# Moving weight loads of a Mamba and FFN layer from SyncE's DMA queue to ScalarE's and GpSimd's

## The reference, cut to what matters

```python
xn = layernorm(x)                                   # 16384 tokens, d_model 1024
# branch 1: a selective state space block, d_inner 2048, 16 states, chunks of 256 tokens
xr = xn @ W_in.T + b_in                             # 1024 -> 4096, split into xc and res
u = silu(causal_conv3(xc) + conv_b)
dlt, Bm, Cm = split(u @ W_x.T, [64, 80])
delta = softplus(dlt @ W_dt.T + b_dt)
carry = exp(delta * -exp(A_log)) * carry + delta * Bm * u     # scan within a chunk, carry 0 at its start
y = sum_over_states(carry * Cm) * silu(res)
ssm = y @ W_out.T + b_out                           # 2048 -> 1024
# branch 2: a gated FFN of 4096, activations rounded to 8 bits, weights to three values
ffn = bitlinear(silu(bitlinear(xn, w_gate)) * bitlinear(xn, w_up), w_down)
out = x + ssm + ffn
```

## Time and profile before

| | |
|---|---|
| time, median of 10 runs | 5199.13 us (5194.39 to 5205.92) |
| time of the profiled execution | 5196.19 us |
| its span on the slowest core (core 0) | 5194.5 us |
| spans of the 8 cores | 5150.0 to 5194.5 us |
| DVE busy | 3800.2 us, 73% of the span |
| ACT, PE busy | 1858.3 us (36%), 1604.3 us (31%) |
| POOL busy | 100.2 us (2%) |
| DMA bytes by queue | SP 316.68 MB, POOL 46.15 MB, ACT 12.58 MB |

### The profile page before, as it was taken

How to read it: one execution, slowest core, us unless ns; L and a number is a source line. 1 busy time by engine, 2 the same in 40 slices (tenths; PEclk the granted TensorE clock), 3 DMA queues, 4 the chain that set the end, 5 groups by cost and what they waited for, 6 DMA issues and landing times.

```text
span 5194.5 us, 46593 instructions; the slowest of 8 cores (5150.0 to 5194.5 us)
## 1 busy us (share of the span) xinstructions
PE 1604.3 (31%) x7308; PEld 812.5 (16%) x7308; DVE 3800.2 (73%) x10735; ACT 1858.3 (36%) x4106; POOL 100.2 (2%) x156
## 2 busy tenths in 40 slices
PE   0134111410321051023104102310200278786776
PEld 0122000200110030012002001200000033333332
DVE  3426888888888888888888888888888566663232
ACT  1335344434443434344333432433223022223342
POOL 0100000000000000000000000000000000000000
PEclk9996555755655575566557556655555699888999
DMA  7532002301400330041004001200100333320666
GB/s 253 159 102 65 1 25 85 106 0 52 135 29 0 105 110 0 28 138 57 0 0 118 1 0 53 65 0 0 49 0 0 106 119 98 105 93 28 212 212 201
DMA packets 311052, 378.37 MB, mean 73 GB/s; under 512 B 15522, under 2 KB 253218, under 8 KB 308644
## 3 DMA queue, kind: packets, MB, share of 16 engines
q1 hardware_dynamic: 296356, 316.68, 20.1%
q0 software_dynamic: 12672, 46.15, 2.5%
q10 hardware_dynamic: 1728, 12.58, 0.8%
HBM read 329.22 MB, written 46.14 MB: 72 GB/s over the span
## 4 chain that ended last, share of the span: by engine, by line
DVE 36%; issue 18%; DMA 17%; PE 16%; ACT 11%; DVEq 1%; SPq 0%; ACTq 0%; POOL 0%; POOLq 0%
DVE hbuf L676 12%; DVE dbub L669 6%; DVE ypb L698 4%; ACT dAb L660 4%; DMA wdqt<-s_wdq 3%; DVE ypb L694 3%; DMA wch<-s_winT 3%; PE psBC L639 2%; PE psI L509 2%; PE psP L1118 2%; DVE yA L701 2%; PE psBC L646 2%; DMA s_wdq<-wdstg 2%; DMA wo_buf<-s_woutT 2%; DMA wqf<-wuT 2%
## 5 line engine op out<-in xcount | busy, mean ns | idle before, releaser
L676 DVE TENSOR_TENSOR_SCAN hbuf<-dAb,dbub 128x256 bf16<-128x256 bf16 x2048 | 1398.5, 683 | 194.3 <-ACT dAb L660 194.0
L660 ACT ACTIVATE dAb<-delta_t,alneg 128x256 bf16<-128x256 bf16 x2048 | 903.3, 500 | 24.5 <-DVE hbuf L676 24.2
L639 PE MATMUL psBC<-shstB,ones 1*128 1x256 f32 x256 | 143.4, 658 | 1955.2 <-DVE shstB L636 1955.2
L650 ACT ACTIVATE Bsb<-psBC 128x256 bf16<-128x256 f32 x128 | 49.0, 383 | 1890.7 <-PE psBC L646 1826.9
L669 DVE TENSOR_TENSOR dbub<-du_t,Bsb 128x256 bf16<-128x256 bf16 x2048 | 579.1, 283 | 6.0 <-ACT Bsb L650 2.4
L701 DVE TENSOR_TENSOR yA<-yA,ypb 128x256 f32<-128x256 f32 x1024 | 435.2, 425 | 109.5 <-DVE ypb L698 4.5
L639 PEld LDWEIGHTS psBC<-shstB,ones 1*128 1x128 f32 x256 | 59.9, 289 | 2009.0 <-issue 2009.0
L509 PE MATMUL psI<-xnsc,wch 128*128 128x256 bf16 x2048 | 305.6, 312 | 152.6 <-DMA wch<-s_winT 130.5
L698 DVE TENSOR_TENSOR ypb<-ypb,pa 128x256 bf16<-128x256 bf16 x896 | 261.6, 292 | 95.6 <-DVE ypb L694 3.2
L694 DVE TENSOR_TENSOR ypb<-hbuf,Csb 128x256 bf16<-128x256 bf16 x1024 | 272.3, 266 | 0.0
L751 PE MATMUL psOut<-wo_buf,gated 128*128 128x512 bf16 x256 | 112.7, 440 | 496.1 <-DVE gated L723 432.1
(11 more groups left out here) (153 smaller groups left out, 3311.0 us busy)
## 6 DMA issues: line engine op xcount, KB each, us to landing
wch<-s_winT SPq DMA_DIRECT2D x128, 512.0 KB, 4.2
wdqt<-s_wdq SPq DMA_DIRECT2D x64, 1024.0 KB, 6.7
wo_buf<-s_woutT SPq DMA_DIRECT2D x64, 512.0 KB, 4.4
wab<-wgT SPq DMA_DIRECT2D x32, 512.0 KB, 3.9
wab<-wuT SPq DMA_DIRECT2D x32, 512.0 KB, 4.3
wab<-wdT SPq DMA_DIRECT2D x32, 512.0 KB, 4.2
wqf<-wgT SPq DMA_DIRECT2D x64, 256.0 KB, 3.4
wqf<-wuT SPq DMA_DIRECT2D x64, 256.0 KB, 3.4
```

Of the source, the lines that this page charges most:

```text
L639: P.op("tensor", lambda t, bk=bk: t.matmul(psBC[bk][:, 0:CH], ones2[64:65, 0:128], shstB[64:65, :], start=True, stop=True), reads=["shB", ...
L660: P.op("scalar", lambda s, q=q, n=n, b=b: s.activation(dAb[b][:], delta_t[p][:, q * CH:(q + 1) * CH], AF.Exp, bias=0.0, scale=alneg[:, q * ...
L676: P.op("vector", lambda v, b=b, b3=b3: v.tensor_tensor_scan(hbuf[b3][:], dAb[b][:], dbub[b3][:], 0.0, ALU.mult, ALU.add), reads=["dA:%d" % ...
```

## The change

Three places name another engine as the issuer of a DMA. The transfers, their sizes, their buffers and everything else stay as they are.

- First stage, weight loads into `wcf`: the even ones go from SP to ACT, the odd ones from ACT to POOL. SP keeps the loads of tokens.
- `wch`: the even loads stay on SP, the odd ones go to POOL.
- `wo_buf`: all 8 of a chunk go from SP to POOL.

```diff
-                    lq = "sync" if wcnt % 2 == 0 else "scalar"
+                    lq = "scalar" if wcnt % 2 == 0 else "gpsimd"
...
-            yield lambda mg=mg, wb=wb: P.op("sync", lambda e: e.dma_start(
-                wch[wb][:].rearrange("part (k c) -> part k c", k=8),
...
+            yield lambda mg=mg, wb=wb: P.op("sync" if mg % 2 == 0 else "gpsimd",
+                lambda e: e.dma_start(
+                    wch[wb][:].rearrange("part (k c) -> part k c", k=8),
...
-                yield lambda kg=kg, f=f, wb2=wb2: P.op("sync", lambda e: e.dma_start(
+                yield lambda kg=kg, f=f, wb2=wb2: P.op("gpsimd", lambda e: e.dma_start(
                     wo_buf[wb2][:].rearrange("part (k c) -> part k c", k=4),
```

More of the change, by code:

```diff
@@ L497, in pre_a_mm @@
             wb = mg % 2
-            yield lambda mg=mg, wb=wb: P.op("sync", lambda e: e.dma_start(
-                wch[wb][:].rearrange("part (k c) -> part k c", k=8),
-                s_winT.ap()[:, mg * 256:(mg + 1) * 256].rearrange(
-                    "(k part) c -> part k c", k=8)),
+            yield lambda mg=mg, wb=wb: P.op("sync" if mg % 2 == 0 else "gpsimd",
+                lambda e: e.dma_start(
+                    wch[wb][:].rearrange("part (k c) -> part k c", k=8),
+                    s_winT.ap()[:, mg * 256:(mg + 1) * 256].rearrange(
+                        "(k part) c -> part k c", k=8)),
                 reads=["swin:%d:0" % k2 for k2 in range(8)],
```

## The result

The changed kernel takes 5347.58 us (median of 8 runs, 5337.39 to 5362.32), 1.0286 times the kernel before, with a 95% interval of 1.0276 to 1.0297. The prediction's 5237 had the direction right; the time lies above its range, 5196 to 5275.

A forecast was written before the change was run, and what follows sets the result against it. DVE was busiest over the span and carried the scan stage's path; loads showed in the first stage. First stage 25.8 + 15 and scan stage 2 made 43 us, less a little, 41: 5237 us, range 5196 to 5275.

The forecast's parts named there:

- The terms 25.8 and 15: First stage: w_inT loads delay cast 7 by 25.8 us; w_outT loads, half of them behind POOL's stores, add 15.
- the lost head start of 28 us: First stage: even load 6, no longer sent ahead by SP, leaves some 28 us later, behind tq0 on ACT.
- The bare chain: First stage: w_inT landings summed load by load, casts and waits included, to 142.8 us for load 7; cast 7 began at 117.04.
- near the even end: Scan stage, wch: an odd load on POOL costs + 0.2 us, within bounds of even and 1.1 us later.
- the other bound: Scan stage, wch: an odd load on POOL comes 1.1 us later, from 0.55 reaction and 0.54 longer issue.
- The even chain is as before: Scan stage, wch: even loads on SP keep their period, landing plus matmuls; only odd ones change, by POOL's price.
- the scan stage's + 50: Scan stage's upper bound: 1.1 us on each of 48 wo_buf loads; 17, a third, entered the range.
- the credit of 12: Scan stage, wo_buf: xnsc and first wch no longer meet the last two wo_buf loads, about 2 us in 6 chunks: - 12.
- the prediction's 10: Scan stage, wo_buf: 48 loads issued when a buffer comes free, + 0.2 us each, + 10 us.
- Rival 1: Scan stage: DVE's work holds up POOL's descriptor writing, loads 1 to 2 us late, 5304 to 5370 us; chance 0.09.
- Rival 2: First stage is bound by bytes and ends as before; scan stage's + 2 remains, 5198 us, no change; chance 0.18.
- Rival 3: Scan stage: wo_buf loads on POOL land 0.7 us sooner, DVE's waits shrink by 40, 5167 us, faster; chance 0.12.

The follow-up runs named there:

- four buffers: Kernel before with four wch buffers instead of two, all on SP, and one gated buffer instead of two: ratio 0.9956, -23 us.
- the fastest kernel: Kernel before with all first-stage loads on SP, three buffers each for wch and wo_buf on SP, one gated buffer: 5162.49 us, ratio 0.9911.
- the split: Kernel before with four wch buffers and one gated buffer, odd wch loads on POOL, even ones on SP: ratio 1.0016, +8 us.
- the filler run: Kernel before with odd wch loads on POOL, plus 16 unused matmuls behind the matmuls of each even load: ratio 1.0261, +136 us.

## Why the prediction was wrong

**First stage: the size held, a reason did not.** The terms 25.8 and 15 came out as 17.8 and 19.3, 41 against 37: one was too high, the other too low, and that the sum is this close is in part luck. What the prediction said of odd loads is what the traces show: they follow the store, and so the cast, of the tile before, and their flight no longer overlaps with that cast. What it said of even loads, that the lost head start of 28 us is part of the cost, the runs do not bear out: without that head start, all on ACT, the time stays within 0.22%, and with it, odd loads on POOL, the loss is larger. The bare chain counted both halves as if each had a price of its own. Why the run with SP's even loads is even slower than the one without is not settled.

**Scan stage, `wch`: the step that failed.** The prediction had 11 us more on PE, of which a third reaches DVE: + 4. PE's waits for `wch` grew by 103.5 us (130.5 to 234.0), and about as much reached DVE: its waits for `dAb` grew by 80.9 and the first `pre_a_mm` by 15.8, 96.7 together. Moved alone, the loads cost 91 us. Five things were wrong in the term.

- The price of a POOL load was taken as + 0.2 us, "near the even end", because of the 3.7 us of the `s_mm` stores. The row that was nearer in kind gave the other bound: the traces show some 0.5 us of reaction and 0.8 of landing, 1.3 for 1.1.
- "The even chain is as before" did not hold: SP's half lands in 5.4 us instead of 4.2.
- The first odd load was priced at 0 because ACT's lead would cover it; it alone costs 31 us.
- The 8 odd loads of the first `pre_a_mm`, with no scan above them, were given no term: 15.8 us.
- "Perhaps a third reaches DVE" had no row. ACT's lead of 26 `dAb` buffers did cover the waits that were there before: with four buffers 114 us of them are gone, and DVE gains next to nothing in the scan (194.0 to 187.1 us of waits for `dAb`). It did not cover what came on top. ACT's list is in order, its evictions of `psI` stand between the `dAb`, and while it waits for PE it produces no decay. These waits of ACT doubled, from 134.3 to 272.8 us (two evictions, before and after):

```profile
ACT sres L544 <- PE psI L509: 76.8, 67, 3.6
...
ACT xc_t L539 <- PE psI L509: 57.5, 50, 4.8
```

```profile
ACT xc_t L540 <- PE psI L510: 144.1, 64, 10.7
...
ACT sres L545 <- PE psI L510: 128.7, 75, 6.8
```

How long a wait the lead covers, no run shows. The upper end of the range left these out too: the scan stage's + 50 held 1.1 us on each `wo_buf` load and nothing for `wch`, and only a third of it went in.

**Scan stage, `wo_buf`: the credit of 12 was not paid.** `xnsc` and the first `wch` do leave before `post_out` now, as forecast (SP issues them at 895.60 and 896.13). But the wait of 3.10 us, which was to be gone with them, is still there:

```profile
988.85 0.38 PE L752 MATMUL psOut<-wo_buf,gated 128*128 128x512 bf16 x1 [3.49 <-DMA wo_buf<-s_woutT]
```

In all, PE waits longer for `wo_buf` than before, 61.3 us against 53.2, so nothing shows that this meeting was what cost there. And POOL in turn sends the next chunk's first `wo_buf` loads too early where nothing stands ahead of them, and the meeting moves to the start of `pre_a_mm`. With `wo_buf` alone on POOL that is some 18 of the 31 us; the other 13 are the six later loads of a chunk. That these are near the prediction's 10 is luck: it had each load 0.2 us later and all of that reaching DVE, while by the traces each lands 0.8 us later after its buffer is free (medians over the 8 cores, 4.46 us from the end of the matmuls to the landing against 3.63) and about a third of it came through. In the whole change the odd `wch` loads stand ahead of these two on POOL and hold them back, which fits the parts adding up to 11 us more than the whole; no run tests that.

**The rivals.** Rival 1's time, 5304 to 5370, holds the result, but its mechanism does not: POOL's `wch` issues took 882 to 918 ns under DVE's work. Only in the first stage did some stretch, and all of them were stores: in the changed kernel one, of 1.78 us from 83.69, ended 0.1 us after a cast on DVE (80.86 + 4.49), and in the run with even loads on SP an `s_xnfm` store again took 2.82 us, issued 0.06 us before a cast. This is the case that the Trainium skill, SBUF — State Buffer, section "SBUF: two separate sides", describes. No odd load stretched, so adding nothing for it was right. Rival 2 named a limit of bytes and had the first stage end as before; it ended 37.1 us later, and the DMA share fell from 0.76 to 0.67 in its first stretch, so time was lost with less asked for, not with more. Rival 3 fails with the credit: DVE's waits for `psOut` grew. The rule cited with rival 2, from DMA: Bandwidth & Descriptors of the Trainium skill, section "Rules for kernel authors", is that issuing from several engines only saves issue time. It agrees with every run here: no run that moved loads to POOL was faster than the same kernel without, and the fastest kernel has all these loads on SP, though it also has more buffers.

**Open: the clock.** In the first `pre_a_mm` PE's work grew from 37.32 us at a granted clock of 0.97 to 44.08 at 0.85, 6.8 of the 15.8 us lost there. With four buffers it was 36.02 on SP and 36.06 with the split, at 1.00 in both. So the slower matmuls go with PE's waits for `wch`; what would happen to the time with the waits and without the lower clock, the filler run did not settle.

## What to carry to other kernels

Before a DMA is moved, write down what stands ahead of it in the new queue and what that waits for, and also what no longer stands ahead of the loads behind it: here an odd load fell in behind two stores, and, with `wo_buf` alone moved, other loads got away some 430 us before their use, into loads that were needed at once. In a chain over two buffers the price of an issuer, reaction and issue and landing, is paid on every load; take it from the nearest row of the same kind, a load that waits on a semaphore. That an engine's lead covers the waits of today does not say that it covers longer ones: here about as much as came on top went through, and where no work stands above the chain, in the first `pre_a_mm`, nothing covered it. Two further buffers hid 60 of the 91 us; the other 31 are as much as the one load behind the stores cost by itself.

## What the runs showed of the hardware that was not expected

- A POOL load of 512 KB in 1024 pieces starts some 0.56 us after the matmuls that free its buffer and takes 0.88 us to issue, and lands in 4.8 to 5.0 us from the start of its issue, where SP's starts within 0.1 us and lands in 4.2.
- While POOL issues half of the loads, SP's half lands later as well: 5.4 us instead of 4.2. With only the first odd load of a chunk on POOL it stays at 4.2. With all loads on POOL they land in 4.8.
- 16 matmuls of 256 columns take 1.91 us at the higher granted clock (2.4 GHz) and 3.57 at the lower (1.2 GHz). In the first `pre_a_mm` the mean granted clock was 1.00, 0.97 and 0.81 with waits for `wch` that grew from one kernel to the next (four buffers, two, two with half of the loads on POOL), and putting 16 more matmuls into every second load did not raise it.
